# A perceiver block on one core: cross attention's end moved from three to four periods ahead of each batch's self attention

## What is computed

```python
x = x + cross_attention(ctx, ctx, norm(x), mask)   # 16 heads of 16, 4096 keys, masked
x = x + top64_attention(norm(x))                   # 16 heads, 256 keys, softmax over the 64 largest scores
x = x + switch_moe(norm(x))                        # 8 experts, capacity 128
x = x + context_attention(norm(x), ctx)            # one head of 256, 4096 keys
x = x + bidirectional_mamba(norm(x))               # 2 directions, 256 channels, 16 states
x = x + tile_ffn(norm(x))                          # 8 tiles, the best one by a sign signature
```

```python
scores = einsum('bhqd,bhkd->bhqk', q, k) / 4
top, idx = top_k(scores, 64)
out = einsum('bhqk,bhqkd->bhqd', softmax(top), v[idx])
```

## Time and profile before

| | before |
|---|---|
| median of 3 runs | 1626.27 us (1622.43 to 1626.83) |
| the profiled execution's own time | 1640.98 us |
| its span | 1639.4 us |
| mean granted TensorE clock | 0.900 |
| PE busy | 1389.7 us, 85% |
| DVE busy | 1250.8 us, 76% |
| ACT busy | 975.8 us, 60% |
| POOL busy | 418.0 us, 25% |

### The profile page before, as it was taken

How to read it: one execution, slowest core, us unless ns; L and a number is a source line. 1 busy time by engine, 2 the same in 40 slices (tenths; PEclk the granted TensorE clock), 3 DMA queues, 4 the chain that set the end, 5 groups by cost and what they waited for, 6 DMA issues and landing times. The chain is left out here.

```text
span 1639.4 us, 31639 instructions
## 1 busy us (share of the span) xinstructions
PE 1389.7 (85%) x11762; PEld 861.7 (53%) x11762; DVE 1250.8 (76%) x3906; ACT 975.8 (60%) x1579; POOL 418.0 (25%) x315
## 2 busy tenths in 40 slices
PE   8999889998999998999967898688859868657746
PEld 4555556665665665666644575366336426423313
DVE  1221189998888997989987899898975785777993
ACT  6778667776675775777752443265564666533530
POOL 4100112232121222222221221222332333333350
PEclk9999999999997997999978899779979988877777
DMA  7745342344202302202105122115354356134230
GB/s 151 171 113 122 79 91 56 76 92 92 29 26 53 53 15 41 53 14 41 40 2 171 52 73 83 52 39 149 117 136 128 98 156 160 59 84 110 65 91 7
DMA packets 96856, 132.68 MB, mean 81 GB/s; under 512 B 20192, under 2 KB 80872, under 8 KB 93744
## 3 DMA queue, kind: packets, MB, share of 16 engines
q1 hardware_dynamic: 96688, 130.50, 32.3%
HBM read 124.95 MB, written 5.51 MB: 80 GB/s over the span
## 5 line engine op out<-in xcount | busy, mean ns | idle before, releaser
L1357 ACT ACTIVATE attn_arena<-ps 128x1024 f32<-128x1024 f32 x512 | 496.5, 1022 | 207.7 <-PE ps L418 206.3
L1951 DVE MATCH_REPLACE8 attn_late<-attn_top,attn_late 128x256 f32<-128x256 f32 x1024 | 411.5, 410 | 0.0
L1948 DVE MAX8 attn_top<-attn_late 128x8 f32<-128x256 f32 x1024 | 381.3, 414 | 23.8 <-ACT attn_late L1379 23.8
L418 PE MATMUL ps<-attn_arena 32*128 32x256 f32 x4096 | 375.5, 410 | 8.1 <-ACT attn_arena L1357 4.3
L418 PEld LDWEIGHTS ps<-attn_arena 32*128 32x128 f32 x4096 | 253.7, 189 | 75.8 <-issue 42.7
L432 PE MATMUL ps<-attn_arena 128*32 128x256 f32 x4096 | 282.4, 393 | 1.4 <-issue 0.7
L1222 POOL TENSOR_SCALAR attn_late<-attn_late 128x512 f32<-128x512 f32 x64 | 95.7, 1495 | 603.1 <-DVE attn_late L1951 603.1
L432 PEld LDWEIGHTS ps<-attn_arena 128*32 128x32 f32 x4096 | 109.0, 110 | 136.3 <-issue 77.2
L693 PE MATMUL ps<-attn_arena 128*128 128x256 f32 x512 | 134.4, 410 | 21.8 <-ACT attn_arena L1459 21.6
L1504 ACT ACTIVATE attn_arena<-attn_late,attn_arena 128x255 f32<-128x255 f32 x256 | 107.9, 496 | 75.3 <-DVE attn_late L1789 36.6
L671 PE MATMUL ps<-attn_arena,attn_q 128*128 128x512 f32 x256 | 134.8, 659 | 17.3 <-ACT attn_arena L1445 11.3
(11 more groups left out here) (237 smaller groups left out, 1578.1 us busy)
## 6 DMA issues: line engine op xcount, KB each, us to landing
attn_arena<-ctxT SPq DMA_DIRECT2D x124, 256.0 KB, 4.8
attn_arena<-maskT SPq DMA_DIRECT2D x32, 512.0 KB, 4.5
attn_arena<-ctx SPq DMA_DIRECT2D x32, 512.0 KB, 4.1
attn_late<-rows SPq DMA_DIRECT2D x256, 64.0 KB, 2.3
attn_arena<-ctxV SPq DMA_DIRECT2D x15, 1024.0 KB, 13.3
attn_late<-wide SPq DMA_DIRECT2D x64, 128.0 KB, 3.0
attn_early<-wide SPq DMA_DIRECT2D x64, 128.0 KB, 3.5
wide<-attn_early SPq DMA_DIRECT2D x16, 256.0 KB, 2.9
```

Of the source, the lines that this page charges most:

```text
L418: mm = pe.matmul(ps[:, first + j - 2 * i, u * S:(u + 1) * S], kx[n % 2][rows, k0:k0 + P], qpad[rows, n % GROUPS, b * S:(b + 1) * S], start ...
L1357: act.activation(probs[m % 2][:, 2 * i:2 * i + 2], ps[:, first:first + 2, :], ACT.Exp, scale=1.0 / 16.0).then_inc(exp_done, 1)
L1948: dve.max(top[:, t, turn], s[:, i, t] if turn == 0 else work[:, i, t]).then_inc(picked, 1)
L1951: dve.match_replace(work[:, i, t], top[:, t, turn], s[:, i, t] if turn == 0 else work[:, i, t], LOW).then_inc(picked, 1)
```

## The change

LEAD is 4 in place of 3. FIRST_P becomes -20 and cross attention spans p = -20 to 43; "ending" has d = 0 at p = -4, 12, 28, 44 in place of -3, 13, 29, 45. For batch 0 (h = 0) the steps of d = 2 stay together in d = 2, period -2, and d = 3 is empty. For h = 1 to 3 the chain of d = 2 is drawn out: DVE adds and normalises in turn 3 of d = 2, PE transposes in slot 3 of d = 2, ACT copies in slot 0 of d = 3, PE makes queries and keys in slot 1 of d = 3, ACT copies them in slot 2, and the first scores are made and copied in slot 3 of d = 3. `make_v` moves from slot 3 to slot 1 of the batch's first period and `add_v` from turn 1 of the next period to turn 4 of this one. DVE's finish of "out", "logits", "h" and "place" moves from turn 1 to turn 3, except for batch 3's (batch 3's "h" and "place" stay in turn 2). `find_bad` on POOL moves behind the roots and the placing of values of its period. Two due times of "h" and two of "xc" move by a period or two slots. All absolute period numbers but these stay.

```diff
--- before.py
+++ after.py
@@ -74,7 +74,7 @@
 N_STATE = 16
 TAPS = 4
 RANK = 8
-LEAD = 3
+LEAD = 4
 FIRST_P = -(H + LEAD)
 CROSS_PER = 4
 GROUPS = H // HG
@@ -90,8 +90,8 @@
 DUE = {
     "ao": [(19, 1), (35, 1), (49, 1), (65, 2)], "out": [(19, 3), (35, 3), (49, 3), (66, 3)],
     "xm": [(21, 1), (37, 1), (51, 3), (67, 2)], "logits": [(23, 3), (39, 3), (52, 3), (68, 3)],
-    "h": [(24, 3), (40, 3), (53, 3), (69, 3)], "place": [(27, 3), (43, 3), (55, 3), (70, 3)],
-    "xc": [(32, 1), (44, 3), (56, 3), (72, 0)], "q": [(36, 1), (48, 1), (57, 1), (72, 2)],
+    "h": [(25, 3), (41, 3), (53, 3), (69, 3)], "place": [(27, 3), (43, 3), (55, 3), (70, 3)],
+    "xc": [(33, 1), (45, 1), (56, 3), (72, 0)], "q": [(36, 1), (48, 1), (57, 1), (72, 2)],
     "o": [(55, 2), (64, 1), (73, 1), (82, 1)], "octx": [(57, 3), (64, 3), (73, 3), (82, 3)],
 }
 SSM_P = [64, 72, 80, 89]
@@ -852,12 +852,16 @@
                         if ending and d == 0:
                             branch["tensor", h] = pe.mark_branch_hint_location()
                             turn_acc(h, GROUPS - 1)
-                        if ending and d == 2:
+                        if ending and d == 2 and h == 0:
                             turn_x(h)
+                        if ending and d == 3 and h:
+                            make_qk(h, 0)
+                        if 0 <= p < B * H and p % H == 0:
+                            make_v(p // H)
                     if slot == 2:
                         if 0 <= done < B * H:
                             products(done)
-                        if ending and d == 2:
+                        if ending and d == 2 and h == 0:
                             make_qk(h, 0)
                     if slot == 3:
                         n = (p - FIRST_P) // CROSS_PER - 1
@@ -868,11 +872,14 @@
                         if ending and d == 1:
                             project(h)
                         if ending and d == 2:
+                            if h:
+                                turn_x(h)
+                            else:
+                                scores(0)
+                        if ending and d == 3 and h:
                             scores(p + 1)
                         if 0 <= p < B * H:
                             b, q = p // H, p % H
-                            if q == 0:
-                                make_v(b)
                             if q in (2, 6, 10):
                                 make_qk(b, (q + 2) // 4)
                     for b in due("ao", p, slot):
@@ -1274,7 +1281,6 @@
                     keep_top(p - 1)
                 if ending and d == 0:
                     branch["pool", h] = pool.mark_branch_hint_location()
-                    find_bad(h)
                 if ending and d == 1:
                     pool.wait_ge(misc_taken, misc["bad", h] + 1)
                     way = pool.value_load(general[0:1, h:h + 1])
@@ -1306,6 +1312,8 @@
                     if b < B - 1:
                         root(roots[0])
                         roots[0] += 1
+                if ending and d == 0:
+                    find_bad(h)
                 if p == CTX_SLOT[0] // CROSS_PER + 3:
                     for i in range(2):
                         pool.memset(decay[i], 0.0).then_inc(ssm_zeroed, 1)
@@ -1542,6 +1550,8 @@
                     elif cross_it(p, slot - 1) == CROSS_ITS - 1 or (slot == 0 and cross_it(p - 1, CROSS_PER - 1) == CROSS_ITS - 1):
                         copy_acc(B * GROUPS - 1)
                     if slot == 0:
+                        if ending and d == 3 and h:
+                            take_misc(xnT.rearrange("p c s -> p (c s)"), M_, "xn", h)
                         if 0 <= p < B * H:
                             soft(p)
                         b, q = p // H, p % H
@@ -1560,22 +1570,20 @@
                             take_pT(done)
                         if ending and d == 1:
                             take_misc(headsT.rearrange("p c s -> p (c s)"), M_, "heads", h)
-                        if ending and d == 2:
+                        if ending and d == 2 and h == 0:
                             take_misc(xnT.rearrange("p c s -> p (c s)"), M_, "xn", h)
                     if slot == 2:
                         if 0 <= p + 1 < B * H and (p + 1) % H:
                             take_scores(p + 1)
-                        if ending and d == 2:
-                            take_sums(done) if done >= 0 else None
+                        if ending and d == (3 if h else 2):
                             take_qk(h, 0)
                     if slot == 3:
+                        if 0 <= done < B * H:
+                            take_sums(done)
                         if ending and d == 0:
-                            take_sums(done) if done >= 0 else None
                             take_misc(general[:, h:h + 1], M_[:, 0:1], "bad", h)
-                        elif ending and d == 2:
-                            take_scores(p + 1)
-                        elif 0 <= done < B * H:
-                            take_sums(done)
+                        if ending and d == (3 if h else 2):
+                            take_scores(H * h)
                     taken = lambda name: due_before(name, p, slot)
                     for b in taken("ao"):
                         take_misc(flat_c(aoT), M_, "ao", b)
@@ -1826,6 +1834,12 @@
                 dve.scalar_tensor_tensor(out=out_y, in0=y_pair(unit)[:, 1], scalar=foh[:, t, 2 * pair + 1:2 * pair + 2], in1=y, op0=ALU.mult, op1=ALU.add).then_inc(y_used, 1)
                 dve.wait_ge(y_used, unit + 1)
 
+            def add_out(b):
+                dve.wait_ge(bo_added, b + 1)
+                add(b, "out")
+                normalise(norms[0], X[:, b * T:(b + 1) * T], xm).then_inc(xm_ready, 1)
+                norms[0] += 1
+
             def between(p, turn):
                 h, d = (p + LEAD) // H, (p + LEAD) % H
                 ending = 0 <= h < B and p + LEAD >= 0
@@ -1847,25 +1861,12 @@
                     n = (p - 1 - FIRST_P) // CROSS_PER - 1
                     if (p - 1 - FIRST_P) % CROSS_PER == 0 and 0 <= n < B * GROUPS and n % GROUPS < GROUPS - 1:
                         divide(n // GROUPS, n % GROUPS)
-                    if p - 1 >= 0 and (p - 1) // H < B and (p - 1) % H == 0:
-                        add_v((p - 1) // H)
                     if 0 <= p - 2 < B * H and (p - 2) % HG == HG - 1:
                         divide_self(p - 2)
-                    for b in due_after("out", p):
-                        dve.wait_ge(bo_added, b + 1)
-                        add(b, "out")
-                        normalise(norms[0], X[:, b * T:(b + 1) * T], xm).then_inc(xm_ready, 1)
-                        norms[0] += 1
-                    for b in due_after("logits", p):
-                        choose(b)
-                    for b in due_after("h", p):
-                        if b < B - 1:
-                            add_bias(b)
-                    for b in due_after("place", p):
-                        if b < B - 1:
-                            add_expert(b)
-                            normalise(norms[0], X[:, b * T:(b + 1) * T], xc).then_inc(xc_ready, 1)
-                            norms[0] += 1
+                    if B - 1 in due_after("out", p):
+                        add_out(B - 1)
+                    if B - 1 in due_after("logits", p):
+                        choose(B - 1)
                     for b in due_after("octx", p):
                         add(b, "octx")
                     if p == SSM_P[0] - 5:
@@ -1903,6 +1904,20 @@
                             normalise(norms[0], X[:, b * T:(b + 1) * T], xc).then_inc(xc_ready, 1)
                             norms[0] += 1
                 if turn == 3:
+                    for b in due_after("out", p):
+                        if b < B - 1:
+                            add_out(b)
+                    for b in due_after("logits", p):
+                        if b < B - 1:
+                            choose(b)
+                    for b in due_after("h", p):
+                        if b < B - 1:
+                            add_bias(b)
+                    for b in due_after("place", p):
+                        if b < B - 1:
+                            add_expert(b)
+                            normalise(norms[0], X[:, b * T:(b + 1) * T], xc).then_inc(xc_ready, 1)
+                            norms[0] += 1
                     for i in passes(-2, p):
                         add_log(i)
                     for b in ffn_batches(11, p):
@@ -1910,6 +1925,8 @@
                     for b in ffn_batches(12, p):
                         ffn_start(b)
                 if turn == 4:
+                    if 0 <= p < B * H and p % H == 0:
+                        add_v(p // H)
                     for i in passes(-4, p):
                         convolve(i)
                 if turn == 5:
@@ -1925,7 +1942,7 @@
                     divide(h, GROUPS - 1)
```

(2 more changed lines are left out.)

## The result

| | before | after |
|---|---|---|
| median of 20 runs each | 1630.75 us (1622.43 to 1650.68) | 1618.01 us (1612.73 to 1623.56) |
| the profiled execution's own time | 1640.98 us | 1618.00 us |
| span | 1639.4 us | 1616.4 us |
| PE, DVE busy | 1389.7, 1250.8 us | 1378.1, 1254.3 us |

The ratio after / before is 0.9945, 95% interval 0.9928 to 0.9962.

The account below looks back on a forecast made before the run. PE and DVE bound the kernel nearly equally, PE setting the pace in periods 17 to 43. The terms sum to -16.2 us on the profiled execution; with only -7 of the clock's -10.2, -13 from 1626.3 gives 1613 us, range 1596 to 1632.

Parts of the forecast that it names:

- batch 1's start: Waits at the addition and ahead of `select(16)` shrink from 9.45 to 3.6 us: -5.9; addition gone from `select(1)`: -0.7.
- period 20: Up to `select(20)`: `make_v` of period 16 ends later than DVE wants it, and PE enters period 17 later, +1.4 us.
- batch 3's start: The wait of 2.05 us in period 44 goes, -2.0, and the 7.48 ahead of `select(47)` go whole, -7.5.
- The extra period: Period -1 delays batch 0's values, so DVE waits in `select(0)` and `select(1)` starts +8.8 us later; bounds 0 and +12.
- batch 2's start: DVE's wait of 7.76 us goes, but PE bounds and the clock falls as before: -2.4 us, from -5 to +5.
- the clock at period 21: An earlier mask ends PE's wait and the clock's fall in period 21: -10.2 us, of which -7 went into the forecast.
- alone that is worth nothing where PE bounds: Removing DVE's wait of 2.17 us in turn 1 of period 20 gains nothing unless the clock's fall goes too.
- `add_v` in period 48: Batch 3's `add_v`, now in turn 4 of period 48, would wait about 4.3 us in place of 3.70: +0.6 us.
- the due times: Moving the due times of "h" and "xc" only shifts work within a period: 0, from -1 to +2 with other edits.
- B: Rival: the clock's fall in period 29 goes too and period 47 runs at full clock: 1600 us, chance 0.21.
- C: Rival: timed runs have no fall at 21 and period 47 costs 7 us, not 3: 1624 us, chance 0.21.
- D: Rival: the clock is low in periods 15, 31, 47, some 9 to 10 us longer each: slower, 1638 us, chance 0.16.

Follow-up runs that it names:

- e4: The changed kernel with the chain of batches 1 to 3 closed up again in d = 2, as batch 0's is: median 1627.2 us, ratio 0.9964 to before.
- second pair: A second trace of the kernel before and of the changed kernel, compared `select` by `select`: -7.5 us at `select(63)`, counted from `select(0)`.
- g2_out0: The kernel before with only batch 0's finish of "out" moved to turn 3 of period 20: median 1623.1 us, ratio 0.9962.
- e3: The changed kernel with DVE's finish put back from turn 3 to turn 1: median 1626.2 us, ratio 0.9957 to before.
- f4: The kernel before, unchanged, executed once more for a second trace: 1628.5 us.
- first pair: The first traces of the kernel before and of the changed kernel, compared `select` by `select`: -26.5 us at `select(63)`, counted from `select(0)`.
- h1: The kernel before with one more period ahead of period 0 and the change's due times of "h" and "xc": median 1642.9 us, ratio 1.0067.
- e1: The kernel before with one more period of cross attention ahead of period 0 and nothing else: median 1651.7 us, ratio 1.0106.
- e2: The kernel before with only DVE's finish of batches 0 to 2 moved from turn 1 to turn 3: median 1622.8 us, ratio 0.9950.
- g3: The kernel before with DVE's finish in turn 3 except batch 0's "out", left in turn 1: median 1628.2 us, ratio 0.9949.

## Why the prediction was right, and where it was not

**Right: the direction, and most of the size.** 1613 was forecast, 1618.0 measured; -13 against -12.7 by the medians of 20 runs, about -9 by the ratio. Three terms hold one by one: batch 1's start (-6.6 with the 0.7 of its values; -6.2 and -4.5), period 20 (+1.4; +1.2), batch 3's start (-9.5; -9.6 and -9.0). The three waits ahead of the addition are gone, and e4, which has them back, loses 7 to 9.6 us by the traces.

**Luck: that -13 and -12.7 lie so close.** The extra period came 3.2 us dearer, batch 2's start 3 to 8 us better and the steps from 47 to 50 some 3 to 5 us better than their terms, and these errors cancel. The profiled execution, for which the sum was made, fell by 23.0 us and not by 16.2, and the second pair by 9.4. The 5 us between 1613 and 1618 come from the start: the three runs shown had a median of 1626.3, twenty have 1630.75.

**Right: the clock at period 21.** The chain "turn 3, so `select(20)` ends 2.2 us sooner, so PE does not starve, so no fall" was forecast with 0.4 us of wait left and a period of 13; g2_out0 has 0.32, the changed kernel 12.67. In the kernel before this is shown; the changed kernel does not need turn 3 for it, as e3 has the wait (2.27 us) and no fall. Carrying part of the -10.2 over to the median was the right use of the gap between the profiled execution and the median; f4 now shows it.

**Mis-sized: the extra period, +8.8, measured +12.0.** The start and the mechanism are as worked out, but I took 8.76 us for a period of cross attention alone and 2.2 for a slot. That row is one of two rhythms. In period -1 two slots take 5.3 us, the period 11.2, though the granted clock is 1.00; the stretch from 150 to 160 us of the same trace runs in the other rhythm. The bound of +12 had the size but not the cause: `soft(0)` runs on ACT at 225.9 us, behind period -1, and by then 2.4 of the 3.2 us are there. The rest are the two slots of period 0. What sets the rhythm is not shown.

**Mis-sized: batch 2's start, -2.4, measured -5.3 and -10.2.** From L582 of period 29 to that of period 30 PE takes 19.5 us in the first trace of before and 15.0 in f4, 15.2 and 16.1 in the two of the changed kernel. So the clock explains 4.4 us of the first pair's -10.2 and none of the second's -5.3. What remains is over 5 us, more than twice the 2.4 that I let through of the wait of 7.76 us at the addition. The wait is not the whole of it: with DVE's finish back in turn 1 (e3) 2.2 and 1.3 us of it return from `select(28)` to 32, by the two traces of the changed kernel; with the chain closed up (e4) 2.9 and 1.9 return up to `select(36)`.

**Wrong: "alone that is worth nothing where PE bounds".** e3 loses 7 to 8 us by the traces with the finish in turn 1 and no fall at 21. The waits of about 2 us on DVE did matter, since they make the mask late on PE, which bounds: 2.27 us ahead of L582 in period 21 against none, and 4.23 against 2.78 in period 29. I had this way in the prediction, but as a cause of the clock's fall only.

**Wrong: `add_v` in period 48 (+0.6) and the due times (0).** `add_v` waits 0 there, against 3.70 before; the 2.03 us ahead of `select(48)` are within what I gave for the chain (+3.0). And h1 against e1 shows 6 to 9 us for the due times: with LEAD at 4 and "h" left at 24 and 40, the change would by that have lost half or more of its gain, though the changed kernel itself was not run so. I had looked for collisions in the changed kernel, where there are none, and not asked what the edit avoids.

**Missed: PE's wait for `find_bad`.** I had it end ahead of PE's question; in period 44, where cross attention is over and PE comes early, PE waits 6.50 us. It cost nothing that the stretches show (-9.6 and -9.0 against -9.5).

The rivals: B's larger gain is seen only in the first pair of traces (and its sum counts 4 us for the rest of the -10.2, where 3.2 are left); C's price for period 47 did not come. D's clock fall did not come in periods 15 and 31; in 47 it did, for 6.8 us in both traces, but `select` 16, 32 and 48 wait 2.0, 3.4 and 2.0 us, not 9.

## What to carry to other kernels

Where two engines are within a few per cent of each other, price a wait by what the other engine does because of it: here 2.2 us on DVE became 2.6 us of idle PE, and with it the lower clock: from one L582 to the next in period 21, 21.1 us in one execution and 14.3 in another, against 12.7 without the wait (g2). Moving that one step two turns later cost nothing, and none of 12 runs was in the tail any more; moving all such steps (e2) gives two thirds or more of what the whole change gives. Here a longer lead cost its whole first period; it paid only with the chain spread over it (7 to 9 us) and the fixed due times moved off the slots that it shifts onto them (6 to 9).

## What the runs showed that was not expected

The same wait of 2.57 us on PE goes with 20.5 us of the lower clock in two executions (the first of before, g3) and 3.4 in another (f4), and period 21 lasts 23.8 us in the first; a wait of 2.27 or 2.28 us there goes with 3.4, 3.4 and none (e1, h1, e3), and the eight traces with at most 0.32 us of wait have no fall in period 21. Period 29 is alike: with a wait of 3.7 us the clock is down for 17.1 us (before, g2) or 6.8 (f4). The stretch from `select(20)` to 24 differs by 7 us between the pairs. One profile prices such a wait only to within that. Cross attention alone, the same instructions, runs at 2.2 or 2.65 us a slot at the same granted clock of 1.00; what decides between the two is not shown.
